# The row stores of the second attention stage, issued from ScalarE's DMA queue in place of SyncE's

## The reference, cut to what matters

```
v = (x @ W_write.T) * beta              # x is the normalised row, d = 128, 2 heads
A = solve_triangular(eye - A0, eye)     # one 37 x 37 system per image and head
o = tril((k @ k.T) * L) @ (A @ v)
h = h + o @ W_read.T                    # the residual row
logits = layernorm(h) @ Wr + br         # the router of the last part
# last part: out = h + gate * expert(layernorm(h))
```

## Time and profile before

| | us |
|---|---|
| median of 3 runs | 1055.56 (1053.3 to 1056.04) |
| the profiled execution, its own time | 1059.34 |
| its span in the trace | 1057.6 |
| the second attention stage, from its first load (706.15) to the start of the next phase (806.89) | 100.7 |
| PE busy over the span | 766.2 (72%) |
| DVE, ACT, POOL busy | 431.8, 242.8, 213.8 |

### The profile page before, as it was taken

One profiled execution on the slowest core, in us unless ns is written; L12 is line 12 of the kernel. 1 busy time (PEld: TensorE's weight loads), 2 busy tenths in 40 slices (PEclk: granted clock), 3 DMA queues, 4 the chain that ended last, 5 costly groups with the idle time before them and its releaser, 6 DMA issues. The chain is left out here.

```text
span 1057.6 us, 16856 instructions
## 1 busy us (share of the span) xinstructions
PE 766.2 (72%) x5266; PEld 612.1 (58%) x5266; DVE 431.8 (41%) x1300; ACT 242.8 (23%) x670; POOL 213.8 (20%) x331
## 2 busy tenths in 40 slices
PE   6999547765775678259999820019771799999995
PEld 4877436654664567248888720018660567667664
DVE  2444313333333333646666630845444233333331
ACT  0000012222222223143433310003330122322321
POOL 2111012222222222003333410003220122222221
PEclk9999855567557655569999955558895699999998
DMA  4444200100000000000000003921224111111110
GB/s 157 132 138 135 59 9 10 10 9 9 9 9 9 9 8 5 1 2 1 0 0 0 0 8 48 435 72 46 65 70 190 40 42 49 45 53 53 46 50 15
DMA packets 65102, 54.11 MB, mean 51 GB/s; under 512 B 51024, under 2 KB 55004, under 8 KB 64550
## 3 DMA queue, kind: packets, MB, share of 16 engines
q1 hardware_dynamic: 55770, 35.70, 12.3%
q0 software_dynamic: 3328, 10.23, 3.3%
q10 hardware_dynamic: 5964, 7.68, 2.2%
HBM read 41.25 MB, written 12.36 MB: 51 GB/s over the span
## 5 line engine op out<-in xcount | busy, mean ns | idle before, releaser
L536 PE MATMUL bank<-cst,arena_w 111*96 111x111 f32 x176 | 37.7, 395 | 95.7 <-DMA arena_w<-q_rows 74.5
L1802 PE MATMUL bank<-arena_w,work 128*128 x208 | 95.2, 601 | 1.0 <-DVE work L1854 1.0
L1826 PE MATMUL bank<-arena_w,work 128*128 x416 | 94.2, 379 | 0.4 <-ACT work L1900 0.4
L248 POOL TENSOR_TENSOR work<-work 111x1 f32<-111x1 f32 x88 | 48.6, 552 | 215.6 <-DVE work L244 215.5
L1900 ACT ACTIVATE work<-bank,cst 128x128 f32<-128x128 f32 x208 | 56.5, 382 | 144.2 <-PE bank L1815 144.2
L1459 PE MATMUL bank<-tokens,work 111*111 (+1 forms) x88 | 17.2, 326 | 99.5 <-POOL work L1428 99.5
L536 PEld LDWEIGHTS bank<-cst,arena_w 111*96 111x96 f32 x176 | 29.8, 196 | 100.7 <-DMA arena_w<-q_rows 79.4
L1826 PEld LDWEIGHTS bank<-arena_w,work 128*128 128x128 f32 x416 | 77.1, 190 | 10.5 <-issue 1.1
L662 DVE TENSOR_REDUCE work<-work 111x16 f32<-111x592 f32 x22 | 16.9, 770 | 136.0 <-ACT work L736 136.0
L316 PE MATMUL bank<-arena_w 128*111 128x256 f32 x264 | 64.7, 397 | 9.1 <-DMA arena_w<-in_pack 9.1
L1459 PEld LDWEIGHTS bank<-tokens,work 111*111 111x111 f32 x88 | 12.9, 204 | 100.8 <-POOL work L1428 87.3
(11 more groups left out here) (211 smaller groups left out, 1428.8 us busy)
## 6 DMA issues: line engine op xcount, KB each, us to landing
arena_w<-in_w SPq DMA_DIRECT2D x2, 4096.0 KB, 13.6
arena_w<-in_x SPq DMA_DIRECT2D x22, 333.0 KB, 3.3
x_rows<-tokens SPq DMA_DIRECT2D x22, 222.0 KB
arena_w<-in_pack ACTq DMA_DIRECT2D x11, 256.5 KB, 4.7
q_rows<-work ACTq DMA_DIRECT2D x22, 111.0 KB
arena_w<-q_rows SPq DMA_DIRECT2D x132, 18.5 KB
cst<-in_packc ACTq DMA_DIRECT2D x11, 157.0 KB, 4.5
arena_w<-in_pack SPq DMA_DIRECT2D x1, 1024.0 KB, 5.8
```

The costliest lines, as they stand in the source:

```text
L248: nc.gpsimd.tensor_tensor(ve[j][:, 1:2], ve[j][:, 0:1], ve[j][:, 2:3], ALU.pow).then_inc(s_rs[j], 1)
L536: mm = nc.tensor.transpose(bank[2 + half][0:KR, k * R:(k + 1) * R], qx[j][:, a:a + KR], ident[0:R, 0:R])
L1802: mm = nc.tensor.matmul(bank[2 * j + f][:, :], xgt[j][:, k * 128:(k + 1) * 128], arena_w1[:, bass.ds(expert * (2 * FF) + (k * FF + f * 512 ...
L1826: mm = nc.tensor.matmul(bank[7][:, 0:D], ht[j][:, g * 128:(g + 1) * 128], arena_w2[:, bass.ds(expert * (FC * D) + g * D, D)], start=(g == ...
```

## The change

SP no longer stores rows. ACT issues each store itself, right behind its copy in `keep_rows`, after a wait that this copy has been written. SP's program keeps the loads and the closing wait for all stores. The transfers are the same ones in number, size and shape.

```diff
--- before.py
+++ after.py
@@ -1396,20 +1396,11 @@
                     sp.dma_start(ac[j].rearrange("p (h t) -> p h t", h=H1),
                                  a_rows[:, bass.ds((2 * i + j) * R, R), :].rearrange("h r t -> r h t")).then_inc(a_in[j], 16)
 
-                def store_rows(pair_at, j):
-                    if pair_at is None:
-                        return
-                    i, n1 = pair_at
-                    sp.wait_ge(x_kept[j], n1)
-                    sp.dma_start(x_rows[bass.ds((2 * i + j) * R + 1, R), :],
-                                 tokens[0:R, bass.ds((2 * i + j) * RW, RW)]).then_inc(x_stored[j], 16)
-
                 def turn(i):
                     for j in range(2):
                         load_inverses(at(sp, i), j)
-                        store_rows(at(sp, i, -3), j)
-
-                run_turns(sp, turn, behind=3)
+
+                run_turns(sp, turn)
                 for j in range(2):
                     sp.wait_ge(x_stored[j], 16 * PAIRS)
 
@@ -1550,6 +1541,9 @@
                     i, n1 = pair_at
                     act.wait_ge(normed[j], n1)
                     nc.scalar.copy(tokens[0:R, bass.ds((2 * i + j) * RW + D, D)], xn[j]).then_inc(x_kept[j], 1)
+                    act.wait_ge(x_kept[j], n1)
+                    act.dma_start(x_rows[bass.ds((2 * i + j) * R + 1, R), :],
+                                  tokens[0:R, bass.ds((2 * i + j) * RW, RW)]).then_inc(x_stored[j], 16)
 
                 def turn(i):
                     before_last, last, this = at(act, i, -2), at(act, i, -1), at(act, i)
```

## The result

The changed kernel took 1062.62 us (median of 3 runs, 1062.45 to 1062.85) against 1055.56 on the same chip: ratio 1.0077, 95% interval 1.004 to 1.0114. It is 7 us **slower**. The forecast of 1054.6 was wrong, and so was the range: 1062.62 lies above its end at 1059.5.

A forecast was written before the change was run, and what follows sets the result against it. Three DMA engines were taken to bound the second attention stage. An earlier first store and turns gave -1.8 to -1.3 us, other terms 0; short gaps made it -1.0, so 1055.56 became 1054.6 us, range 1050.5 to 1059.5.

The forecast's parts named there:

- What bounds the stage: Second attention stage: three DMA engines work without pause, 3.81 us per tile, while PE would need 2.78.
- six stores always stood behind the loads: SP's queue before the change: waiting stores gave the DMA engines work at every moment.
- First store earlier, -1.8 us: ACT issues the first store at about 718.9, not 720.67; engines start at 720.4 instead of 722.2: -1.8 us.
- ACT's queue uses the same three engines: Stores on ACT's queue use the same three DMA engines as SP's, so no DMA work is removed.
- The rival of separate engines: ACT's queue has other DMA engines, stage runs at PE's 2.78 us a tile: 16.7 us earlier, 1038.9; chance 0.08.
- ACT's wait and issue, 0 us: ACT's 22 added issues and waits for its own copy fit its idle time: 0 us.
- A load beside stores takes 6.8 us: If two queues alternate by packet, a load's 74 packets per engine at 92 ns take 6.8 us beside waiting stores.
- Last spread later: Sign of being right: POOL's last spread comes later than 784; with turns the last load lands at 789.7.
- The same 22 stores ... 0 us: Main term: the stage's 22 stores and 22 loads keep their shapes, so 0 us of DMA work is removed.
- 3.3 us for slow packets and gaps: Of 81.1 us from first store data to 803.3, 77.8 is engine work; the remaining 3.3 was carried over.
- engines that never run dry: Condition for the -1.8 to -1.3 us sum: the three DMA engines always have work; one or two short gaps expected.
- The rival of dry engines: Slow loads clear all stores, leaving both queues empty up to 2.3 us at a time: +4.7 us, 1060.3; chance 0.16.

The follow-up runs named there:

- e8: Kernel before (SP stores), each store cut into two transfers of 96 and 15 rows: 1028.18 us against 1049.79, ratio 0.9785.
- e1: Kernel before, SP still storing the rows; ACT also waits for its copy and issues a 4-byte transfer: ratio 1.0001 to before.
- e7: Changed kernel (ACT stores), each store cut into two transfers of 96 and 15 rows: ratio 0.9846 to before.
- e9: Kernel before, each of SP's last six stores also waiting until the previous one landed: 1065.22 us, one run.
- e2: Changed kernel with a_rows laid out so a load is 111 runs of 296 bytes, not 222 of 148: ratio 1.0093 to before.
- e5: Changed kernel with four load buffers instead of two, SP's and POOL's turns written out, a semaphore per buffer: ratio 1.0031 to before.
- e10: Changed kernel with eight load buffers instead of two, SP's and POOL's turns written out, a semaphore per buffer: ratio 0.999 to before.
- e4: Kernel before, SP storing each tile two turns behind the load instead of three: ratio 1.0079 to before.
- e11: Kernel before with SP storing two turns behind instead of three, four load buffers, turns written out, a semaphore per buffer: ratio 1.0026 to before.
- e3: Changed kernel with ACT issuing each store two turns (four tiles) later: ratio 1.0163 to before.

## Why the prediction was wrong, step by step

- *What bounds the stage:* right for the kernel before. Three engines do the work, and e8 shortens the stage to 72.6 us by using more of them. But that "six stores always stood behind the loads" was a misreading: they stood in SP's program, and at each load one or two of them had been copied.
- *First store earlier, -1.8 us:* right, and somewhat small. It was issued 715.21 - 702.48 = 12.7 us into the stage, before 14.5. Its first data moved 0.8 us later and not 1.5. No load stood ahead of it in ACT's queue, and three later stores that found this queue empty took 0.8 us as well (issued at 731.21, 766.05 and 784.37). So the data began to move 13.5 us into the stage against 16.1, 2.6 us earlier.
- *ACT's queue uses the same three engines:* right. The rival of separate engines is out, with the share at 0.20.
- *ACT's wait and issue, 0 us:* right for this kernel (e1: 1.0001; issue 0.26 us, 0.03 us behind the copy). My note that they would fit even at PE's pace of 2.78 us was tested with two issues per tile, and there it did not hold (e7 against e8).
- *A load beside stores takes 6.8 us:* right. 732.07 - 725.46 = 6.61 and 760.59 - 753.88 = 6.71.
- *Last spread later:* right in direction, short in size. Forecast 789.7 - 706.15 = 83.6 us into the stage, measured 86.5. The sum behind it goes on with 789.9 where it had found 789.7; this is 0.2 us and changes nothing.
- *"The same 22 stores ... 0 us", with its 3.3 us for slow packets and gaps carried over, and "engines that never run dry": this step failed.* From the first 2 KB packet to the end of the last it took 82.8 us before and 92.1 after: 9.3 us more, less the 2.6 of the earlier start is +6.7, the whole loss. Slow packets make 6.7 of the 9.3 (10.9 us per engine after, 4.2 before; in e1, the same stage as before, 1.1). Stretches with fewer than three packets in flight make 1.6 (2.9 against 1.3).
- *The rival of dry engines* had the right direction, and its 1060.3 is nearer than the forecast. I had worked out that two slow loads clear the queue of stores, and gave it 0.16, with five events of 1.2 us. But it priced an empty queue by the time it is empty, and this is the small part. The windows under a share of 0.15 that were to be the sign are three of 1 us (766:767, 789:790, 793:794). The large part is that a store which comes to an empty queue starts slowly (e9). A third part may be PE: at the clock of 0.50 it does 8 matmuls in 2 us, at 1.00 it does 15 (742:744 and 748:750 above), and so makes the next stores later.
- *The chances:* the reasoning gave turns by packet as the likely behaviour and the empty queue as its consequence. A rival that follows from the forecast's own mechanism deserved more than the forecast without it.

Shown: the turns (packet records, e2), no cost of ACT's issue (e1), that the loss goes when loads are asked for earlier (e5, e10), the price of an empty queue (e9, one run), and that one queue loses as much once its stores come late (e4, e11). Not settled: what PE's clock adds, since no run changed it by itself; why a store on an empty queue starts slowly; and whether two queues would lose anything if their stores came in time, since e3 started too late to tell.

## What to carry to other kernels

Moving transfers to another queue added no DMA engine here (a share of 0.20 after, 0.21 before); it changed who goes first, and the load of many small packets lost most against the large ones, since turns went by packet: 6.6 to 6.7 us in place of 0.86 alone. Three DMA engines bound this stage, and stores issued 3.1 us or more before the ones ahead of them ended kept them full (4.2 us of slow packets; 10.9 where eight were issued less than 1.3 us before, or behind): before a reorder, ask what refills the queue after it is cleared. And before arranging three engines better, look at the number of rows: 96 + 15 instead of 111 was worth 2.15%, more than any order of queues lost here.

## What the runs showed of the hardware

- In this stage the two queues alternate packet by packet, 2 KB against 148 bytes: 69 packets of each queue in 2 us (724:726 of the kernel after), at most two of one queue in a row. The first phase had looked otherwise, where small loads lost nothing beside ACT's store, 142 packets in 1 us with it and without; why is open.
- A store on an empty queue starts slowly: in e9 it moved 31 KB in its first half microsecond and then 37, 55 and 76 GB/s, against a steady 77 with stores queued behind each other (794:798 before). That is 0.9 us lost for this store, and 0.9 us of slow packets for each of the last five.
- PE's granted clock after waits: in the window 724:726 of the kernel after PE did nothing and the granted clock was 0.50; in 758:760 it did nothing either and the clock was still 1.00, to be 0.50 in 762:764. Over 717:789 it was 0.76. In 730:760 of e7 and e8, with PE at 78% and 96% busy, it was 1.00.
- A DMA issue took 0.25 to 2.25 us on SP before and 0.26 to 0.29 on ACT after, with up to three stores outstanding. Where more stood in ACT's queue it was longer there too: up to 1.29 us in e10 and 2.99 at the end of e3. That the length of the queue sets it is my reading; no run varied it alone.
